# Layer 0's first attention pass written out by itself, and the second group's weights split inside iteration 0

## The chip, the cores and the metric

One core of one Trainium2 chip runs the whole kernel in one launch. The metric is device time in microseconds (us); lower is better. PE is TensorE, DVE VectorE, ACT ScalarE, POOL GpSimd, and SP the engine that issues most transfers. Every engine takes its own instructions strictly in order and waits on semaphores.

## What is computed

Two transformer layers over 4 x 256 tokens of width 256 and a context of 4 x 1601. The change lies in layer 0's attention. Cut to what matters:

```python
ln_out = _ln(hidden_states, ln_w, ln_b)
q  = _ln(fp8_linear(ln_out, wq).reshape(b, s, g, hpg, d))     # 8 groups, 2 heads each, d = 128
k  = _ln(fp8_linear(ln_out, wk).reshape(b, s, g, d))
v  = fp8_linear(ln_out, wv)
core = _gqa(q, k, v)
qx = _ln(fp8_linear(ln_out, wqx).reshape(b, s, g, hpg, d))
kx, vx = split(cond @ w_kv_x.T)                               # 1601 context rows
xout = _gqa(qx, _ln(kx), vx)
catq = _div_clamp_fp8(concatenate([core, xout]), proj_smooth)
out  = (catq @ wproj.T) * (proj_in_scale * proj_w_scale)
```

`fp8_linear` rounds its input to fp8; float32 factors are carried as a high and a low bf16 part.

## The kernel before

Layer 0's attention is 32 iterations (`NGB`), one for each pair of group and batch. The first 16 alternate between batches 0 and 1, so iterations 0 and 1 use group 0, and 2 and 3 use group 1. In iteration `it` the kernel makes the scores and probabilities of `it` and, between them, prepares `it + 1`: queries (`Q0`, `Q1`), keys (`K0` to `K3`), transposed queries (`TQ0`, `TQ1`), sums of squares of the keys (`SS`) and values (`V0` to `V3`). It also multiplies the probabilities of the iteration before by its values. An iteration "-1" has the same order with nothing but the preparation for 0, and work of the start is put between: rounding of the inputs to fp8 (rounds `j` = 0 to 7, four for each of two batches), the split of the second batch's context, and the split of group 1's weights.

Weights. Group 0's lie in `wsb`. Group 1's raw weights `wf1` are split by ACT (high parts, L737), DVE (low parts, L638) and POOL (the context's keys and values, L553 and L555) into `wo`. SP stores `wo` to `w_split` in device memory (`sp_store_weights`, L446), and later loads it into `wsb` in three pieces (`load_weights`, L972): keys (256 KB) and queries (512 KB) for the next iteration but one, values later. PE's first work of iteration 1 is `Q0` of iteration 2, which waits for the piece of the queries:

```python
elif i == 0:
    if new_group(it):
        e.wait_ge(s["ld_q"], 16 * (groups_taken(it) - 1))
```

The load of iteration 2 in turn waits for the store, `e.wait_ge(s["w_out"], 32)`.

The keys' norms. ACT copies `SS` out and issues a small transfer into `ssc`; POOL takes the power -1/2 (`key_norm`, L1110); SP writes that row to device memory (`row_out`, L989) and, once it has landed, reads it back spread over all partitions (`row_in`, L1002), which DVE's scaling of the scores (L1298) needs. SP's other work is the DMA transpose of the probabilities (`turn_p`, L1017).

Rounding. ACT scales (L785), DVE clips and takes exponents (L661, L665, L667) and adds (L672), and DVE or POOL subtracts (L677, L539).

Buffers. PE's products of the preparation go through three banks, `pa` and two of `tb`; `wait_bank` makes a product wait for the reader of the one three slots earlier.

Of the kernel before, what the change touches and what calls it, by code (L numbers as in the profile page):

```python
# [127 lines left out]
def allocate(nc, m, whole):  # L128
# [36 lines left out]
    with ExitStack() as attn:  # L165
# [7 lines left out]
        with ExitStack() as c:  # L173
# [15 lines left out]
            sb(c, "free_turned", [P, IC, NT * P - S], F32)  # L189
            m.wf[1] = sb(c, "wf1", [P, IC, WCOLS], F32)  # L190
            m.wo = sb(c, "wo", [P, 2 * IC * WCOLS], BF16)
        with ExitStack() as c:
# [33 lines left out]
            m.yq = [sb(c, f"yq{i}", [P, 512], BF16) for i in range(2)]  # L226
            m.ye = sb(c, "ye", [P, 512], BF16)
            m.ym = [sb(c, f"ym{i}", [P, 512], BF16) for i in range(2)]
            m.yt = sb(c, "yt", [P, 512], F32)
# [2919 lines left out]
```

## Time and profile before

| | us |
|---|---|
| median of 3 runs | 1675.77 (1675.32 to 1676.99) |
| the profiled execution, and its span | 1673.28, 1671.5 |
| PE busy in the span | 1593.3 (95%) |
| DVE, ACT, POOL busy | 1389.5 (83%), 1387.6 (83%), 1142.2 (68%) |
| PE's first product of iteration 0 (`Q0` of 1) starts at | 59.41 |
| PE busy up to there | 24.24 |
| PE's first product of iteration 1, of 2 and of 3 | 91.00, 123.70, 159.54 |

Times within the trace count from the span's start. "r" in the prediction is time since the start of iteration 0 on PE. A row of the timeline gives start, duration, engine, line, operation, output<-input, shapes and a count; in square brackets is the idle time ahead of it and what ended that.

### The profile page before, as it was taken

What the parts mean: (1) busy time and instruction counts of PE and PEld (TensorE: products, weight loads), DVE (VectorE), ACT (ScalarE), POOL (GpSimd) and SP (SyncE); (2) the same over time, 40 slices, a digit from 0 to 9 for tenths busy, and PEclk for the clock granted to TensorE, in tenths of its full rate; (3) what the DMA queues carried; (4) which work ended last, traced back from release to release, by engine and by line L of the source; (5) the groups of instructions that cost most, each with busy time, mean ns of one, the idle gap of its engine ahead of it and who ended that gap; (6) DMA issues with size and microseconds to landing.
All of it is one profiled execution on the core that took longest, in us unless ns stands there. A gap on an engine that the chain in (4) does not pass through costs nothing. (4 is left out here: it accounts for less than half of the span.)

```text
span 1671.5 us, 44071 instructions
## 1 busy us (share of the span) xinstructions
PE 1593.3 (95%) x15996; PEld 1000.8 (60%) x15996; DVE 1389.5 (83%) x3486; ACT 1387.6 (83%) x2346; POOL 1142.2 (68%) x1775
## 2 busy tenths in 40 slices
PE   3799999999999999999999999998898999999998
PEld 1566777767777677777777677776554333333333
DVE  7899999999999989999988999899896755655422
ACT  6688888888887888888888888885347999999997
POOL 3668778687787777888788888876775655646300
PEclk9899999999999999999999999999999999999999
DMA  5399989899998998999999999999333222222100
GB/s 180 90 200 204 193 197 197 188 203 207 212 192 200 220 208 186 221 217 218 211 196 206 214 210 209 200 182 249 116 51 112 46 54 70 41 40 47 33 14 14
DMA packets 609481, 261.12 MB, mean 156 GB/s; under 512 B 576624, under 2 KB 581744, under 8 KB 607856
## 3 DMA queue, kind: packets, MB, share of 16 engines
q1 hardware_dynamic: 605040, 258.05, 71.6%
q8 instruction: 127, 2.08, 0.5%
q10 hardware_dynamic: 4224, 0.25, 0.2%
q14 instruction: 90, 0.74, 0.1%
HBM read 99.15 MB, written 17.29 MB: 70 GB/s over the span
## 5 line engine op out<-in xcount | busy, mean ns | idle before, releaser
L1815 PE MATMUL score<-KK,QT 128*128 128x512 bf16 (+2 forms) x1920 | 340.7, 321 | 8.1 <-DVE mxp L1298 7.5
L1835 PE MATMUL pv<-PT,VV 128*128 128x256 bf16 (+1 forms) x2880 | 338.8, 274 | 6.5 <-DMA PT<-PB 6.0
L1569 ACT ACTIVATE PB<-S,rsum 128x1024 bf16<-128x1024 f32 (+1 forms) x256 | 246.2, 987 | 109.2 <-DVE rsum L1329 85.0
L1835 PEld LDWEIGHTS pv<-PT,VV 128*128 128x128 bf16 (+1 forms) x2880 | 279.7, 98 | 72.9 <-issue 32.7
L1320 DVE SCALAR_TENSOR_TENSOR PB<-S,rsum,PB 128x1024 bf16<-128x1024 f32 (+1 forms) x256 | 292.2, 1142 | 0.3 <-ACT PB L1569 0.3
L1815 PEld LDWEIGHTS score<-KK,QT 128*128 128x128 bf16 x1920 | 157.0, 98 | 146.8 <-DVE mxp L1298 16.8
L1559 ACT ACTIVATE S<-S,nmx 128x1601 f32<-128x1601 f32 x128 | 210.0, 1641 | 6.4 <-DVE nmx L1310 6.3
L2884 ACT ACTIVATE P<-score 128x1024 f32<-128x1024 f32 x196 | 197.7, 1052 | 1.7 <-PE score L2976 0.8
L2996 PE MATMUL pv<-P,V 128*9 128x256 f32 (+1 forms) x2288 | 152.2, 380 | 1.1 <-DVE pv L2267 0.8
L1694 PE MATMUL tb<-stage,wsb 128*128 128x512 bf16 (+1 forms) x768 | 148.1, 335 | 4.7 <-DVE stage L645 3.9
L1127 POOL TENSOR_SCALAR S<-S,rsum 128x256 f32<-128x256 f32 x128 | 74.4, 581 | 108.8 <-DVE rsum L1329 101.8
L1149 POOL TENSOR_TENSOR catq<-yt,ym 128x512 bf16<-128x512 f32 x64 | 114.9, 1795 | 0.3
L1298 DVE CUSTOM_DVE_ANT_0 S<-score,x 128x1024 f32<-128x1024 f32 (+1 forms) x128 | 104.4, 816 | 6.5 <-PE score L1815 4.5
L1298 DVE CUSTOM_DVE_ANT_0 S<-score,rsb 128x1024 f32<-128x1024 f32 (+1 forms) x128 | 104.5, 816 | 6.2 <-PE score L1815 2.9
L1694 PEld LDWEIGHTS tb<-stage,wsb 128*128 128x128 bf16 x768 | 66.2, 98 | 70.0 <-issue 6.6
L1513 ACT ACTIVATE kn<-pa,a_nm,a_rs 128x128 f32<-128x128 f32 x256 | 95.7, 455 | 8.0 <-POOL a_nm L1090 8.0
L1085 POOL TENSOR_SCALAR a_nm<-a_mv 128x4 f32<-128x4 f32 x64 | 41.8, 653 | 88.3 <-DVE a_mv L1264 88.3
L1735 PE MATMUL tb<-wsb,stage 128*128 128x128 bf16 x1536 | 98.7, 222 | 3.0 <-DVE KK L1231 2.8
L1139 POOL TENSOR_TENSOR yt<-yq,ym 128x512 f32<-128x512 bf16 x64 | 91.4, 1428 | 14.4 <-DVE ym L1354 9.6
L1131 POOL TENSOR_TENSOR PB<-S,PB 128x256 bf16<-128x256 f32 x128 | 90.3, 705 | 10.9
L1735 PEld LDWEIGHTS tb<-wsb,stage 128*128 128x128 bf16 x1536 | 93.2, 99 | 7.2 <-DVE KK L1231 5.2
L2976 PE MATMUL score<-QB,KT 32*128 32x256 bf16 (+1 forms) x1110 | 91.0, 274 | 4.5 <-ACT P L2884 2.5
(295 smaller groups left out, 3671.7 us busy)
## 6 DMA issues: line engine op xcount, KB each, us to landing
x<-rs_d SPq DMA_DIRECT2D x16, 936.0 KB, 5.2
rsb<-rs_d SPq DMA_DIRECT2D x16, 936.0 KB, 5.5
wsb<-w_split SPq DMA_DIRECT2D x46, 256.0 KB, 4.7
wsb<-w_split SPq DMA_DIRECT2D x23, 512.0 KB, 4.9
wpr<-in_wprojT SPq DMA_DIRECT2D x23, 512.0 KB, 6.6
context_d<-stage SPq DMA_DIRECT2D x16, 400.2 KB, 4.1
l_ctx<-context_d SPq DMA_DIRECT2D x4, 1601.0 KB, 7.3
rawh<-in_w_all SPq DMA_DIRECT2D x12, 512.0 KB, 5.5
```

The source lines that it names most:

```text
L1149: e.tensor_tensor(out[:, :, pr * 256:(pr + 1) * 256], m.yt[:, :].rearrange("p (k c) -> p k c", k=2), m.ym[pr][:, :].rearrange("p (k c) -> ...
L1298: e.tensor_tensor_reduce(m.S32[par][:, at:at + b - a], m.score[:, a:b], m.rsb[it % 2][:, key:key + b - a], 1.0, start, ALU.mult, ALU.max, ...
L1320: e.scalar_tensor_tensor(m.PB[n % 2][:, lo:lo + b - a], m.S32[n % 2][:, a:b], m.rsum[n % 2][:, 1:2], m.PB[n % 2][:, 2 * a:a + b], ALU.mult ...
L1513: a = e.activation(m.kn[i][:, k * D:(k + 1) * D], bank[:, k * D:(k + 1) * D], ACT.Identity, bias=m.anm[i][:, k:k + 1], scale=m.ars[i][:, k ...
L1559: e.activation(x, x, ACT.Exp, bias=m.nmx[par][:, 1:2], accum_out=m.sums[par][:, 1:2])
L1569: e.activation(m.PB[n % 2][:, 2 * a:a + b], m.S32[n % 2][:, a:b], ACT.Copy, scale=m.rsum[n % 2][:, 1:2]).then_inc(s["p_hi"], 1)
L1694: r = e.matmul(bank[:, 0:b - a], wk[:, w, ic, D:2 * D], ctx_op(m, it, part, ic, a, b), start=(n == 0), stop=(n == 5))
L1735: r = e.matmul(bank[:, h * D:(h + 1) * D], ctx_op(m, it, part, ic, t * P, (t + 1) * P), wv[:, w, ic, D:2 * D], start=(n == 0), stop=(n == 5))
L1815: i = e.matmul(m.score[:, at:at + b - a], qt[:, kind, qp, q * P:(q + 1) * P], kk[:, kp, a:b], start=(k == 0), stop=(k == 2))
L1835: i = e.matmul(m.pv[:, at:at + 256], vv[0:rows, v, t, :], m.PT[k % 2][0:rows, turned(c, a), :], start=(c == first and r == 0), stop=(c == ...
L2884: e.activation(pr[:, :], bank, ACT.Exp, scale=float(D1) ** -0.5).then_inc(s["l1_exp"], 1)
L2996: r = e.matmul(m.pv[j * R:j * R + VC, 0:S], m.V1[p][0:rows, t, 4 * hq + j, :], probabilities(m, n, j // 2)[0:rows, at:at + S], start=(t == ...
```

## The change

Iteration -1 goes. In its place each engine has a list of its own for the first pass. ACT and DVE split both halves of the first context before they scale or round any input. PE makes `K0` and `K1` first, then `Q0`, `K2`, `K3`, transposes the rest of the tokens, and puts `SS` directly behind the keys; POOL's root and the row's way over device memory follow. Rounds 5, 6 and 7, and the whole split of group 1's weights, move into iteration 0. SP stores `wo` there behind the row of iteration 1, and then loads iteration 2's keys' and queries' weights. Four small buffers move in the memory map, since `wo` now lives longer; waits in iteration 1 guard their first use. The core of the diff:

```diff
@@ allocate
+            m.yq = [sb(c, f"yq{i}", [P, 512], BF16) for i in range(2)]
+            m.ye = sb(c, "ye", [P, 512], BF16)
+            m.ym = [sb(c, f"ym{i}", [P, 512], BF16) for i in range(2)]
+            m.yt = sb(c, "yt", [P, 512], F32)
             m.ast = [sb(c, f"a_st{i}", [P, 4, 6], F32) for i in range(2)]
...
@@ pool_prologue
+    for i in range(2):
+        e.memset(m.S32[i][:, SC:SELFC], 0.0).then_inc(s["p_pad"], 1)
...
+    pool_round_end(e, m, s, 1)
@@ dve_prologue
     dve_weights_low(e, m, s, 0, 1)
-    dve_round(e, m, s, 0)
     dve_context_low(e, m, s, 0, 0)
-    dve_round(e, m, s, 1)
     dve_context_low(e, m, s, 0, 1)
-    dve_weights_low(e, m, s, 0, 2)
     e.wait_ge(s["x_rest"], 16)
     dve_statistics(e, m, s, 1, m.x, TB, NT)
...
+    dve_round(e, m, s, 0)
@@ act_prologue
+    act_context_high(e, m, s, 0, 0)
+    act_context_high(e, m, s, 0, 1)
     act_scaled_inputs(e, m, s, 0)
-    act_context_high(e, m, s, 0, 0)
     act_scaled_inputs(e, m, s, 1)
-    act_context_high(e, m, s, 0, 1)
     act_weights_high(e, m, s, 0, 2)
-    act_scaled_inputs(e, m, s, 2)
     act_weights_high(e, m, s, 0, 3)
-    act_scaled_inputs(e, m, s, 3)
...
+FIRST = ("K0", "K1", "Q0", "K2", "K3", "SS", "TQ0", "V0", "Q1", "V1", "TQ1", "V2", "V3", "PR")
...
-    at = ORDER.index(what)
+    at = (ORDER if it else FIRST).index(what)
@@ sp_attention
-    for it in range(-1, NGB + LAG - 1):
-        if it == -1:
-            sp_store_weights(e, m, s, 1)
-        if it == 0:
-            sp_small(e, m, s)
+    row_out(0)
+    row_in(0)
+    sp_small(e, m, s)
+
+    for it in range(NGB + LAG - 1):
...
-        load_weights(it + 2, 0)
+        if it:
+            load_weights(it + 2, 0)
...
-        if it + 2 < PAIRS:
+        if 0 < it < PAIRS - 2:
             load_weights(it + 2, 1)
         row_out(it + 1)
         row_in(it + 1)
+        if it == 0:
+            sp_store_weights(e, m, s, 1)
...
         turn_p(4 * it + 1, 1)
+        if it == 0:
+            load_weights(2, 0)
+            load_weights(2, 1)
@@ pool_attention
-    for it in range(-1, NGB + LAG - 1):
-        if it == 0:
-            e.wait_ge(s["xq_done"], 8)
...
+    query_norm(0, 0)
+    pool_round_end(e, m, s, 2)
+    pool_context_low(e, m, s, 1, 0)
+    key_norm(0)
+    query_low(0, 0)
+    query_norm(0, 1)
+    pool_round_end(e, m, s, 4)
+    pool_context_low(e, m, s, 1, 1)
+    query_low(0, 1)
+
+    for it in range(NGB + LAG - 1):
...
+        if it == 0:
+            pool_round_end(e, m, s, 5)
+            pool_split_weights(e, m, s, 1, 0)
+            pool_round_end(e, m, s, 6)
         split_self(4 * it)
         query_norm(it + 1, 1)
         query_low(it + 1, 0)
-        if it == -1:
-            pool_split_weights(e, m, s, 1, 0)
-            pool_round_end(e, m, s, 4)
+        if it == 0:
+            pool_round_end(e, m, s, 7)
             pool_split_weights(e, m, s, 1, 1)
...
         key_norm(it + 1)
...
+        if it == 1:
+            e.wait_ge(s["w_out"], 32)
@@ dve_attention
+        if it == 0:
+            dve_round_start(e, m, s, 5)
+            dve_round_add(e, m, s, 5)
...
+        if it == 0:
+            dve_round_start(e, m, s, 6)
+            dve_round_add(e, m, s, 6)
+        if it == 1:
+            e.wait_ge(s["w_lo_pool"], 8)
...
+        if it == 0:
+            dve_weights_low(e, m, s, 1, 0)
         invert(4 * it)
...
+        if it == 0:
+            dve_weights_low(e, m, s, 1, 1)
...
+        if it == 0:
+            dve_round_start(e, m, s, 7)
+            dve_round_add(e, m, s, 7)
...
+        if it == 0:
+            dve_weights_low(e, m, s, 1, 2)
+            dve_weights_low(e, m, s, 1, 3)
         values_low(it + 1, 0)
@@ act_attention
+    keys_high(0, 0)
+    act_scaled_inputs(e, m, s, 2)
+    keys_high(0, 1)
+    act_normalise_rest(e, m, s)
+    keys_high(0, 2)
+    keys_high(0, 3)
+    act_scaled_inputs(e, m, s, 3)
+    query_norm(0, 0)
+    act_context_high(e, m, s, 1, 0)
+    sums_out(0)
+    query_full(0, 0)
...
+        if it == 0:
+            act_scaled_inputs(e, m, s, 6)
...
+        if it == 0:
+            act_weights_high(e, m, s, 1, 0)
+            act_scaled_inputs(e, m, s, 7)
...
+        if it == 0:
+            act_weights_high(e, m, s, 1, 1)
         p_hi(4 * it, 0)
...
+        if it == 0:
             act_weights_high(e, m, s, 1, 2)
             act_weights_high(e, m, s, 1, 3)
+        query_norm(it + 1, 1)
@@ pe_attention
+        if n == 0 and half == 0:
+            e.wait_ge(s["xw_done"], 2 * IC)
...
+    keys(0, 0)
+    keys(0, 1)
+    queries(0, 0)
+    keys(0, 2)
+    keys(0, 3)
+    pe_turn_normed(e, m, s, 1)
+    squares(0)
+    turn_queries(0, 0)
+    values(0, 0)
+    queries(0, 1)
+    values(0, 1)
+    turn_queries(0, 1)
+    values(0, 2)
+    values(0, 3)
```

PE's order at the start of the program, before. `score<-ident,xn` is the transposition of normalised tokens, `pa<-wsb,stage` queries, `tb<-stage,wsb` keys, `tb<-sq,ones` the sums of squares, `tb<-wsb,stage` values:

```order
L831 MATMUL score<-ident,xn 128x128 x4
L1768 MATMUL pa<-wsb,stage 128x256 x8
L1694 MATMUL tb<-stage,wsb 128x512 x12
L831 MATMUL score<-ident,xn 128x128 x12
L1779 MATMUL pa<-ident,kn 128x128 x4
L1694 MATMUL tb<-stage,wsb 128x512 x6
L1694 MATMUL tb<-stage,wsb 128x65 x6
L1702 MATMUL tb<-stage,wsb 128x256 x4
L1768 MATMUL pa<-wsb,stage 128x256 x8
L1716 MATMUL tb<-sq,ones 32x480 x4
L1735 MATMUL tb<-wsb,stage 128x128 x48
```

And of the change:

```order
L825 MATMUL score<-ident,xn 128x128 x4
L1725 MATMUL tb<-stage,wsb 128x512 x12
L1799 MATMUL pa<-wsb,stage 128x256 x8
L1725 MATMUL tb<-stage,wsb 128x512 x6
L1725 MATMUL tb<-stage,wsb 128x65 x6
L1733 MATMUL tb<-stage,wsb 128x256 x4
L825 MATMUL score<-ident,xn 128x128 x12
L1747 MATMUL tb<-sq,ones 32x480 x4
L1810 MATMUL pa<-ident,kn 128x128 x4
L1766 MATMUL tb<-wsb,stage 128x128 x24
L1799 MATMUL pa<-wsb,stage 128x256 x8
```

The keys moved ahead of the queries, and the squares ahead of the second queries and of all transposed queries and values.

SP's order from the store of group 0's weights on, before (`x<-rs_d` and `rsb<-rs_d` are the rows of iterations 0 and 1 read back):

```order
L446 DMA w_split<-wsb 128x4096
L446 DMA w_split<-wo 128x4096
L989 DMA rs_d<-rr 128x15
L1002 DMA x<-rs_d 128x1872
...
L972 DMA wsb<-w_split 128x1024
L1017 DMA_TRANSPOSE PT<-PB 128x14x128
L1017 DMA_TRANSPOSE PT<-PB 128x16x128 x2
L972 DMA wsb<-w_split 128x2048
L989 DMA rs_d<-rr 128x15
L1002 DMA rsb<-rs_d 128x1872
L1017 DMA_TRANSPOSE PT<-PB 128x14x128
```

And of the change, up to where iteration 1's transposes begin:

```order
L446 DMA w_split<-wsb 128x4096
L984 DMA rs_d<-rr 128x15
L997 DMA x<-rs_d 128x1872
...
L1012 DMA_TRANSPOSE PT<-PB 128x14x128
L1012 DMA_TRANSPOSE PT<-PB 128x16x128 x2
L984 DMA rs_d<-rr 128x15
L997 DMA rsb<-rs_d 128x1872
L446 DMA w_split<-wo 128x4096
L1012 DMA_TRANSPOSE PT<-PB 128x14x128
L967 DMA wsb<-w_split 128x1024
L967 DMA wsb<-w_split 128x2048
```

The store of `wo` moved from ahead of iteration 0's row to behind iteration 1's, and both loads of `wsb` moved behind the store.

POOL's order from the second queries' norm of iteration 1 to the root of its keys, before (`wo` and `acc` are the split weights of groups 1 and 2, `stage<-late,ex` the end of a round, `rr<-ssc,mhalf` the root):

```order
L1090 TENSOR_TENSOR a_nm<-a_nm,a_rs 128x4
L1099 CAST QT<-t 128x512
L1101 TENSOR_TENSOR QT<-t,QT 128x512
L553 CAST acc<-rawh 128x128
L555 TENSOR_TENSOR acc<-rawh,acc 128x128
...
L1131 TENSOR_TENSOR PB<-S_1,PB 128x256
L1110 TENSOR_TENSOR rr<-ssc,mhalf 128x15
```

And of the change:

```order
L1091 TENSOR_TENSOR a_nm<-a_nm,a_rs 128x4
L1100 CAST QT<-t 128x512
L1102 TENSOR_TENSOR QT<-t,QT 128x512
L539 TENSOR_TENSOR stage<-late,ex 128x512
L553 CAST wo<-wf 128x128
L555 TENSOR_TENSOR wo<-wf,wo 128x128
L553 CAST wo<-wf 128x128
L555 TENSOR_TENSOR wo<-wf,wo 128x128
L553 CAST acc<-rawh 128x128
L555 TENSOR_TENSOR acc<-rawh,acc 128x128
...
L1132 TENSOR_TENSOR PB<-S_1,PB 128x256
L1111 TENSOR_TENSOR rr<-ssc,mhalf 128x15
```

One end of a round and one part of the split of `wo` now stand between the queries and the root.

## Rows read from the trace of the kernel before

**Rows 1.** Windows: busy time by engine in iterations 0 and 1, then clock, DMA.
```profile
59.41:91.00 31.59, 27.18 (x230) 17.64 (x231) 26.83 (x79) 25.82 (x61) 18.26 (x29) 0.95 0.54 122
91.00:123.70 32.70, 32.59 (x299) 23.31 (x297) 29.92 (x76) 27.14 (x53) 18.48 (x24) 1.00 1.00 204
```

**Rows 2.** Timeline, PE: first keys, a value, first queries of iterations 0, 1.
```profile
21.86 4.16 PE L1694 MATMUL tb<-stage,wsb 128*128 128x512 bf16 x12 [3.94 <-DVE stage L645]
...
49.10 2.74 PE L1735 MATMUL tb<-wsb,stage 128*128 128x128 bf16 x24 [0.20 <-ACT sqs L1534]
...
59.41 1.89 PE L1768 MATMUL pa<-wsb,stage 128*128 128x256 bf16 x8 [4.00 <-DVE VV L1244]
...
91.00 1.04 PE L1768 MATMUL pa<-wsb,stage 128*128 128x256 bf16 x8
```

**Rows 3.** Groups of lines, ACT, 0 to 62.3 us.
```profile
L765 ACT CAST stage<-cf 128x1601 bf16<-128x1601 f32 x4 | 6.1, 1524 | 0.0
L785 ACT ACTIVATE stage<-xr,rin 128x256 bf16<-128x256 f32 x8 | 3.6, 504 | 0.0
...
L737 ACT ACTIVATE wo<-wf,win 128x256 bf16<-128x256 f32 (+1 forms) x8 | 3.1, 461 | 0.0
L793 ACT ACTIVATE xn<-x,rr,rs 128x256 f32<-128x256 f32 x6 | 3.1, 587 | 0.7 <-POOL rr L586 0.7
L1513 ACT ACTIVATE kn<-pa,a_nm,a_rs 128x128 f32<-128x128 f32 x8 | 3.0, 457 | 3.3 <-POOL a_nm L1090 3.3
```

**Rows 4.** The landing times of the contexts' transfers (`cf`).
```profile
DMA to landing us min/median/max: 4.2/5.5/8.2
```

**Rows 5.** Groups of lines, POOL, 0 to 62.3 us.
```profile
L562 POOL TENSOR_TENSOR stage<-cf,stage 128x577 bf16<-128x577 f32 x4 | 5.7, 1428 | 5.0 <-ACT stage L765 5.0
L539 POOL TENSOR_TENSOR stage<-late,ex 128x512 bf16<-128x512 f32 x3 | 3.5, 1154 | 1.0 <-DVE late L672 1.0
L1110 POOL TENSOR_TENSOR rr<-ssc,mhalf 128x15 f32<-128x15 f32 x1 | 2.7, 2749 | 0.0
L1101 POOL TENSOR_TENSOR QT<-t,QT 128x512 bf16<-128x512 f32 x2 | 2.4, 1182 | 0.2
L1088 POOL TENSOR_TENSOR a_rs<-a_rs,mhalf 128x4 f32<-128x4 f32 x2 | 2.2, 1080 | 0.2
...
L555 POOL TENSOR_TENSOR wo<-wf,wo 128x128 bf16<-128x128 f32 x4 | 2.1, 516 | 0.3
```

**Rows 6.** Groups of lines, DVE, 0 to 62.3 us.
```profile
L672 DVE TENSOR_TENSOR late<-stage,ex 128x512 f32<-128x512 bf16 x8 | 5.5, 693 | 0.3
...
L638 DVE SCALAR_TENSOR_TENSOR wo<-wf,win,wo 128x256 bf16<-128x256 f32 (+1 forms) x8 | 4.1, 556 | 0.0
```

**Rows 7.** Timeline, ACT, in iteration 0.
```profile
64.57 0.69 ACT L1485 ACTIVATE KK<-tb,dcols 128x512 bf16<-128x512 f32 x1 [7.78 <-PE tb L1694]
65.15 0.59 ACT L1490 ACTIVATE sq<-tb 128x512 f32<-128x512 f32 x1
...
72.03 1.86 ACT L1569 ACTIVATE PB<-S,rsum 128x1024 bf16<-128x1024 f32 x2
```

**Rows 8.** Timeline, DVE: statistics of the second queries in iteration 0.
```profile
73.75 0.89 DVE L1258 BATCH_NORM_STATS2 a_st<-pa 128x6 f32<-128x128 f32 x4 [0.58 <-PE pa L1768]
```

**Rows 9.** Timeline, POOL: root of iteration 1's keys.
```profile
84.09 2.76 POOL L1110 TENSOR_TENSOR rr<-ssc,mhalf 128x15 f32<-128x15 f32 x1
```

**Rows 10.** Timeline, SP's queue: row of iteration 1 out and in.
```profile
86.88 0.32 SPq L989 DMA_DIRECT2D rs_d<-rr  x1
90.38 0.32 SPq L1002 DMA_DIRECT2D rsb<-rs_d  x1
```

**Rows 11.** DMA issues, 0 to 100 us: size, us to landing.
```profile
w_split<-wo SPq DMA_DIRECT2D x1, 1024.0 KB, 3.9
...
rsb<-rs_d SPq DMA_DIRECT2D x1, 936.0 KB, 5.4
...
wsb<-w_split SPq DMA_DIRECT2D x1, 512.0 KB, 4.4
```

More of the change, by code:

```diff
@@ L225, in allocate @@
             m.rsum = [sb(c, f"rsum{i}", [P, 2], F32) for i in range(2)]
[L226 to L229, printed above, removed]
             m.rawh = sb(c, "rawh", [P, IC, 512], F32)[:, :, :]
@@ L1150, in take_magnitudes @@
                         m.ym[pr][:, :].rearrange("p (k c) -> p k c", k=2), ALU.subtract).then_inc(s["yq_done"], 1)
-    for it in range(-1, NGB + LAG - 1):
-        if it == 0:
-            e.wait_ge(s["xq_done"], 8)
-            for i in range(2):
-                e.memset(m.S32[i][:, SC:SELFC], 0.0).then_inc(s["p_pad"], 1)
+    query_norm(0, 0)
[8 more added lines that the diff above has]
+    for it in range(NGB + LAG - 1):
         query_norm(it + 1, 0)
@@ L1355, in exponents @@
                         ALU.add).then_inc(s["y_mag"], 1)
-    for it in range(-1, NGB + LAG - 1):
+    keys_low(0, 0)
+    dve_round_start(e, m, s, 1)
+    dve_round_add(e, m, s, 1)
+    keys_low(0, 1)
+    query_stats(0, 0)
+    dve_weights_low(e, m, s, 0, 2)
+    dve_round_start(e, m, s, 2)
+    dve_round_add(e, m, s, 2)
+    keys_low(0, 2)
+    keys_low(0, 3)
+    dve_weights_low(e, m, s, 0, 3)
+    dve_round(e, m, s, 3)
+    e.tensor_scalar(m.gate[:, 0:1], m.gate[:, 0:1], sc(m, "pw"), sc(m, "pin"), ALU.mult, ALU.mult)
+    e.reciprocal(m.rsmc[:, :], m.smc[:, :])
+    dve_context_low(e, m, s, 1, 0)
+    dve_sum_weights(e, m, s, 1)
+    dve_centre_weights(e, m, s, 1)
+    query_stats(0, 1)
+    values_low(0, 0)
+    dve_round_start(e, m, s, 4)
+    dve_round_add(e, m, s, 4)
+    values_low(0, 1)
+    dve_context_low(e, m, s, 1, 1)
+    values_low(0, 2)
+    values_low(0, 3)
+    for it in range(NGB + LAG - 1):
         query_stats(it + 1, 0)
@@ L1570, in p_hi @@
             s["p_hi"], 1)
-    for it in range(-1, NGB + LAG - 1):
+    keys_high(0, 0)
[9 more added lines that the diff above has]
+    query_full(0, 0)
+    for ic in range(IC):
+        act_norm_weighted(e, m, s, ic)
+    act_scaled_inputs(e, m, s, 4)
+    values_high(0, 0)
+    values_high(0, 1)
+    act_context_high(e, m, s, 1, 1)
+    query_norm(0, 1)
+    query_full(0, 1)
+    values_high(0, 2)
+    values_high(0, 3)
+    act_scaled_inputs(e, m, s, 5)
+    for it in range(NGB + LAG - 1):
         if it == 0:
             e.wait_ge(s["p_pad"], 3)
-            e.wait_ge(s["w_lo_dve"], 16)
-            e.wait_ge(s["w_lo_pool"], 8)
+            e.wait_ge(s["w_lo_dve"], 8)
+            e.wait_ge(s["w_lo_pool"], 4)
             e.wait_ge(s["ctx_lo_dve"], 2 * IC)
             e.wait_ge(s["ctx_lo_pool"], 2 * IC)
-            e.wait_ge(s["xq_done"], 8)
         p_hi(4 * it - 1, 0)
         keys_high(it + 1, 0)
-        if it == -1:
-            act_context_high(e, m, s, 1, 0)
-            act_normalise_rest(e, m, s)
+        if it == 0:
+            act_scaled_inputs(e, m, s, 6)
         if it < NGB - 1:
@@ L1837, in times_v @@
         i.then_inc(s["tv_done"], 1)
-    for it in range(-1, NGB + LAG - 1):
+    keys(0, 0)
[12 more added lines that the diff above has]
+    values(0, 3)
+    for it in range(NGB + LAG - 1):
         queries(it + 1, 0)
```

66 lines of the change are left out of this document (3 added, 63 removed).

## The prediction

> **What bounds the kernel now.** I read the windows first. From iteration 1 on PE is the bound: it is busy 32.59 of 32.70 us there [rows 1], so whatever moves the start of iteration 1 moves the end by as much. Two stretches are not PE's: everything up to 59.41, where PE's first product of iteration 0 starts [rows 2], and iteration 0 itself, where PE works 27.18 of 31.59 us and DVE 26.83, ACT 25.82 [rows 1]. The time before is thus 59.41 + 31.59 + the rest, and the whole question is when `Q0` of iteration 2, which starts at 91.00 [rows 2], can start now. Next I read the timelines of both stretches, engine by engine, and last the transfers, because the code makes that product wait for one.
>
> **The first pass: when does iteration 0 start?** No duration changes, so I lay the new lists out by hand along the chain that ends last.
> - Contexts. The later of them lands 8.2 us after its issue at about 4.1 to 4.5 [rows 4], so at 12.5. The cast takes 1.5 [rows 3] and POOL's upper half of the low part 1.4 [rows 5]: `K0` starts at 15.4, where it started at 21.86 [rows 2]. `K0` and `K1` take 4.2 together [rows 2], to 19.6.
> - ACT then has `K1`'s high part and square (0.7 and 0.6 [rows 7]) to 20.9, the normalisation of the other tokens 3.1 [rows 3] to 24.0, two more pairs for `K2` and `K3` (2.3) to 26.3, a scaling 0.9 [rows 3] to 27.2, the queries' norm 1.5 and a context's cast 1.5 [rows 3] to 30.2, and the copy of the sums, about 0.6 as one such square, to 30.8. (This last row is the one that used to come behind the second queries.)
> - The small transfer of the sums lands some 2.5 later: such a row took at most 3.5 from its issue until the next could go [rows 10], and I take a little less. POOL's root takes 2.75 [rows 5]: 33.3 to 36.0.
> - POOL then writes the first queries (0.6 + 1.2, by the cast's half and the row of 1.18 [rows 5]) to 37.8 and takes the root for the second (a power of 1.08 [rows 5] and three tiny ones, 2.0) to 39.8. ACT normalises them by 41.3, PE transposes, ACT scales, and PE's third value of up to 2.74 [rows 2] ends near 44.4; its high and low part take 0.6 and 0.7.
> This puts `Q0` of iteration 1 at 45.3: 14.1 us earlier than 59.41. The value at the higher clock gives 44.5, a slower context (5.5 from its issue is the median, 8.2 the slowest, so it is not likely) or 1 us of contention on POOL 47. POOL and ACT are both nearly full between 20 and 40, so I don't expect less than 44.
>
> **Iteration 0 gets longer.** Moved in are, on ACT, two scalings (3.6 us for four [rows 3], so 1.8) and the high parts of `wo`, 3.1 [rows 3]; on DVE, three rounds of four steps, 0.69 for the last [rows 6] and near 1.0 for the other three, 1.7 each, less the round of 2.4 that ran at its start, and the low parts, 4.1 with contention [rows 6]; on POOL, three ends of rounds at 1.15 and two splits at 1.7 (0.52 and about 0.35, twice [rows 5]). ACT was idle 7.78 us, but only until `K0` of iteration 1 [rows 7], and nothing that moved stands there but one scaling: the rest lies behind it, where ACT had no gap.
> - ACT reaches the high parts of the probabilities, which began at r = 72.03 - 59.41 = 12.6 [rows 7], after two scalings and two parts of the weights: 0.9 + 0.9 + 0.9 + 0.7 = 3.4 later, r 16.0.
> - DVE's low part of the second piece waits for ACT just ahead of that, to r 16. Its statistics of the second queries, at r 14.3 [rows 8], then come at r 18.3: 4.0 later.
> - POOL's root of iteration 1's keys hangs on those statistics through a chain without a gap. It ended at 84.09 + 2.76 = 86.85, r 27.4 [rows 9]. Now 4.0 later for DVE, and an end of a round (1.15) and a split (1.7) stand ahead of it: r 34.3; I take 33.8, for some contention falls away.
> - PE itself would reach `Q0` of iteration 2 at r 37.5, where it was at 31.6: the values wait for DVE's last low part of the keys, which waits for ACT.
> So without any transfer in the way iteration 0 costs 5.9 more and the change wins 14.1 - 5.9 = 8.2 us.
>
> **But the reload is late.** Before, both pieces of `wsb` were loaded during iteration 0. Now SP issues, in this order: the row out behind the root, the row in, the store of `wo`, a transpose, and only after the store has landed the keys' and queries' weights. From the end of the root, K = 45.3 + 33.8 = 79.1:
> - row out to row in: 3.5 [rows 10]
> - row in to the store's issue: 0.4; the store alone lands in 3.9 [rows 11], but 936 KB of the row, 5.4 us to landing [rows 11], go ahead of it through the same DMA engines. It lands between 3.9 and about 7 after its issue (5.4 and some 2 for its own bytes); I take 5.9.
> - two issues, 0.4 for the second; the 512 KB of the queries' weights land in 4.4 [rows 11], with the transpose ahead of them.
> Sum: 3.5 + 0.4 + 5.9 + 0.4 + 4.4 = 14.6, between 12.6 with the store alone and 15.7 with the row and 7.0 for the store; a transpose of some 2 us in front gives 18. `Q0` of iteration 2 starts at 79.1 + 14.6 = 93.7. PE would be ready at 45.3 + 37.5 = 82.8 and stands still for 10.9 us. Queued behind that product are all of iteration 1's scores, so nothing fills the hole. 93.7 - 91.0 = 2.7 later than before.
>
> The Trainium skill (DMA: Bandwidth & Descriptors, "Anatomy of one DMA") puts a transfer at 2.0 us fixed and its bytes at 436 GB/s. By this estimate row, row and store together, and both loads take 2.0 + 0.4 + 6.6 + 0.4 + 3.8 = 13.2 instead of 14.6, and the sum of the change would be 1.4 less; for the store alone it gives 4.4, where the trace has 3.9 [rows 11], and no row shows a store behind a row. The same page's rules for kernel authors ask that a transfer be issued early and waited for late; this change does the opposite with the store and the loads.
>
> **The clock.** After 4.0 us idle the eight products at 59.41 took 1.89, and at 91.00, behind a busy PE, 1.04 [rows 2]: 0.85 lost in that group alone. After 10.9 us idle the slow stretch is longer; two to three times 0.85 is 1.7 to 2.6. I take 1.8.
>
> Sum: +2.7 + 1.8 = +4.5 us. The other edits cost nothing: the waits of iteration 1 are for things then long done (the store landed before PE could go on), the memsets moved into POOL's idle start. The profiled execution took 1673.28, 2.5 below the median; its terms hold for both. Median 1675.77 + 4.5 = 1680.3.
>
> **Rivals.**
> 1. The reload is in time (faster): the change does what its first pass promises. It needs the queries' weights landed by 82.8, when PE comes; from `Q0` at 91.0 - 1.8 - 3.4 = 85.8 on it is no longer measurably faster. It would happen if POOL's root came at once with its sums (spans on POOL are rough, and it has 13 us idle of 31.59 before [rows 1]): K at r 26, 71.3, and the short chain of 12.6 give 83.9. Against it: POOL's list puts two splits and a round ahead of the root. 1667.6 at best, 1671 in the middle.
> 2. A wash: the store lands in its 3.9 beside the row, and K is 1 us early: 78.1 + 12.6 = 90.7, -0.3 + 1.8 = +1.5, 1677.3. For it: DMA engines are half idle in iteration 0 (0.54 [rows 1]). Against it: the row and the store follow within 0.4 us.
> 3. Worse: the transpose and the row both hold the path, 18 us from K, and iteration 0 starts at 46.5: 98.3, +7.3 + 2.6 = +9.9, 1685.7.
> 4. The stall gives something back: ACT, DVE and the DMA catch up in it, and PE's few waits of iterations 2 and 3 vanish. At most 1 to 2 us, since PE was busy 32.59 of 32.70 just behind [rows 1]; it is inside the range.
>
> **How the numbers follow.** Forecast (stall of about 11 us, +2.5 to +7): 0.50. Rival 2 (-3 to +2.5): 0.26. Rival 3: 0.08. Rival 1: 0.16. A change of 0.2% (3.4 us) is about what can be told from none. The likeliest case alone runs from 1678 to 1683. The range takes in rival 2 and parts of 1 and 3: 1671.5 to 1686. Slower by over 0.2%: two thirds of the forecast's case and more, and rival 3: 0.52. Within: 0.31. Faster: 0.17.
>
> **What would show it.** PE's first keys near 15.4 and the squares near 28; `Q0` of iteration 1 near 45; POOL's root of iteration 1 near 79; an idle of 8 to 14 us ahead of PE's `Q0` of iteration 2, ended by the transfer `wsb<-w_split`, at 92 to 96; the lower clock behind it; from there on the same distances as before. The prediction is wrong if that idle is under 3 us, or if iteration 0 starts later than 49.

## The result, and the profile after

The changed kernel takes 1681.54 us (median of 6 runs, 1678.66 to 1683.66) where the kernel before took 1675.34 beside it (6 runs, 1673.41 to 1676.99). The ratio is 1.0037, with a 95% interval of 1.0027 to 1.0048: slower by 6.2 us. The profiled execution has a span of 1679.6 us.

The windows of the first pass, of iteration 0 and of iteration 1 (span of the window, busy time of PE, PEld, DVE, ACT and POOL, granted clock, DMA share, GB/s), which answer to [rows 1]:

```profile
0.00:47.65 47.65, 20.87 (x162) 14.20 (x163) 37.02 (x97) 30.31 (x58) 29.08 (x53) 0.93 0.50 190
47.65:96.08 48.43, 28.90 (x230) 18.36 (x231) 35.48 (x98) 34.77 (x81) 27.41 (x37) 0.80 0.44 104
96.08:130.90 34.82, 34.81 (x296) 24.16 (x297) 27.68 (x70) 23.48 (x47) 18.99 (x24) 0.93 0.73 145
```

The first pass is 11.76 us shorter than its 59.41 [rows 2]. Iteration 0 is 16.84 longer than its 31.59, iteration 1 2.12 longer than its 32.70 [rows 1]. Both engines that took on work are far from full in iteration 0 (ACT 34.77 of 48.43 us), so it is not their load that fills it. TensorE's timeline has the reason (start, busy time, then in brackets the idle time ahead and what ended it), against [rows 2]:

```profile
16.62 5.28 PE L1725 MATMUL tb<-stage,wsb 128*128 128x512 bf16 x12 [8.69 <-POOL stage L562]
...
42.60 1.09 PE L1810 MATMUL tb<-ident,kn 128*128 128x128 f32 x4 [6.14 <-ACT kn L1536]
...
47.65 1.05 PE L1799 MATMUL pa<-wsb,stage 128*128 128x256 bf16 x8 [0.54 <-DVE VV L1249]
...
96.08 1.86 PE L1799 MATMUL pa<-wsb,stage 128*128 128x256 bf16 x8 [11.75 <-DMA wsb<-w_split]
97.74 2.76 PE L1848 MATMUL score<-KK,QT 128*128 128x512 bf16 x6
100.30 1.76 PE L1725 MATMUL tb<-stage,wsb 128*128 128x512 bf16 x6
```

The rows at 47.65 and 96.08 are `Q0` of iterations 1 and 2. TensorE is through with everything else at 96.08 - 11.75 = 84.33, which is 6.7 us earlier than it was at this place before, and then stands still for the weights. After the pause the same products run at about half speed (six scores take 2.76 instead of 1.46). From `Q0` of iteration 3 on, at 130.90, the distances are those of before: `Q0` of iteration 5 stands at 201.44, against 194.32.

SP's queue in iteration 0 shows the chain in front of that load, and the landings of its transfers (size, median us from issue to landing) what it is made of; compare [rows 10, 11]:

```profile
80.70 0.36 SPq L984 DMA_DIRECT2D rs_d<-rr  x1
82.16 0.33 SPq L997 DMA_DIRECT2D rsb<-rs_d  x1
82.65 0.32 SPq L446 DMA_DIRECT2D w_split<-wo  x1
83.07 5.62 SPq L1012 DMA_TRANSPOSE PT<-PB  x1
90.86 0.80 SPq L967 DMA_DIRECT2D wsb<-w_split  x2
...
w_split<-wo SPq DMA_DIRECT2D x1, 1024.0 KB, 8.1
rsb<-rs_d SPq DMA_DIRECT2D x1, 936.0 KB, 6.1
...
wsb<-w_split SPq DMA_DIRECT2D x1, 512.0 KB, 4.7
```

The store of `wo` leaves at 82.65 and lands 8.1 us later; alone, before the change, it landed in 3.9 [rows 11]. Only then may the loads go.

And POOL's last piece of `wo`, and the root that SP's row waits for:

```profile
74.06 0.49 POOL L555 TENSOR_TENSOR wo<-wf,wo 128x128 bf16<-128x128 f32 x1
...
77.87 2.80 POOL L1111 TENSOR_TENSOR rr<-ssc,mhalf 128x15 f32<-128x15 f32 x1
```

POOL's share of the split is ready at 74.6, DVE's at 75.0. So the store stands for over 7 us behind the row in SP's list, with its data ready. SP's waits between 60 and 100 us name the root as what the row waited for; the root ends at 80.67 and the row leaves at 80.70:

```profile
SPq L984 <- POOL rr L1111: 3.2, 1, 3.2
```

### The profile page after: what moved, and what is told of

Its sections match the earlier page's. It is cut to its first block and busy times, and to the rows that moved or that the text cites. A ratio compares the mean times of both kernels' runs of the same rounds, so it can differ in the third digit from the quotient of the medians.

```text
span 1679.6 us, 44073 instructions
## 1 busy us (share of the span) xinstructions
PE 1595.2 (95%) x15996; PEld 1001.1 (60%) x15996; DVE 1384.2 (82%) x3483; ACT 1386.4 (83%) x2346; POOL 1151.1 (69%) x1778
## 5 line engine op out<-in xcount | busy, mean ns | idle before, releaser
L1508 ACT ACTIVATE KK<-tb,dcols 128x512 bf16<-128x512 f32 (+1 forms) x128 | 76.1, 594 | 31.1 <-PE tb L1725 31.1
L1132 POOL TENSOR_TENSOR PB<-S,PB 128x256 bf16<-128x256 f32 x128 | 93.6, 731 | 10.9
```

## Experiments

Theory A: the chain row, store, loads in front of iteration 2's first queries is the loss; without it the first pass's gain would come through, less what iteration 0 has taken on. Rivals: TensorE would wait for something else there (B); iteration 0 is too long by its new work (C); the new first pass is worth little by itself (D).

All kernels side by side. `Q0(1)` and `Q0(2)` are the starts of those queries in the profiled execution, "wait" is TensorE's idle time ahead of the second; iteration 1 is from `Q0(2)` to `Q0(3)`. The ratio is against the kernel before on the same chip.

| kernel | Q0(1) | Q0(2) | wait | iteration 1 | median us | ratio, 95% interval |
|---|---|---|---|---|---|---|
| before | 59.41 | 91.00 | 0 | 32.70 | 1675.34 | 1 |
| changed | 47.65 | 96.08 | 11.75 | 34.82 | 1681.54 | 1.0037 [1.0027, 1.0048] |
| e1 store early | 47.66 | 91.89 | 7.25 | 34.97 | 1676.86 | 1.0007 [0.9998, 1.0016] |
| e10 and loads ahead of row_in | 48.75 | 90.97 | 4.79 | 34.87 | 1675.50 | 0.9995 [0.9986, 1.0005] |
| e2 copies inside SBUF | 48.79 | 85.28 | 0 | 35.61 | 1669.67 | 0.9963 [0.9951, 0.9976] |
| e4 second store | 47.49 | 98.10 | 13.98 | 35.04 | 1683.60 | 1.0054 [1.0039, 1.0069] |
| e5 root first | 48.87 | 97.44 | 11.55 | 34.79 | 1682.05 | 1.0036 [1.0023, 1.0049] |
| e3 split in the first pass | 48.72 | 83.17 | 0 | 32.32 | 1667.84 | 0.9952 [0.9939, 0.9964] |
| e6 and rounds 5 to 7 too | 49.64 | 84.97 | 0 | 32.31 | 1667.78 | 0.9954 [0.9942, 0.9967] |
| e7 is e3, norm first | 48.12 | 81.97 | 0 | 32.31 | 1664.54 | 0.9935 [0.9923, 0.9948] |
| e8 is e7, keys first | 47.96 | 82.97 | 0 | 32.41 | 1664.83 | 0.9931 [0.9918, 0.9945] |
| e11 is e6, norm first | 49.20 | 85.64 | 0 | 32.31 | 1666.95 | 0.9951 [0.9939, 0.9963] |
| e9 76 products in the wait | 48.88 | 97.67 | 3.79 | 34.00 | 1684.51 | 1.0058 [1.0044, 1.0073] |
| e12 104 products in the wait | 48.96 | 98.17 | 0.22 | 32.71 | 1684.18 | 1.0067 [1.0048, 1.0086] |

**e1, the store early.** In iteration 0 of SP's list:

```diff
+        if it == 0:
+            sp_store_weights(e, m, s, 1)
         row_out(it + 1)
         row_in(it + 1)
         if it == 0:
-            sp_store_weights(e, m, s, 1)
+            load_weights(2, 0)
+            load_weights(2, 1)
...
         turn_p(4 * it + 1, 1)
-        if it == 0:
-            load_weights(2, 0)
-            load_weights(2, 1)
```

> Only SP's order in iteration 0 changes: the 1 MB store of the second group's weights goes ahead of row_out(1), and the two loads for iteration 2 directly behind row_in(1), ahead of the fourth transpose. Theory A (the chain row, store, loads holds TensorE for 11.75 us in front of iteration 2's first queries, and with the lower clock behind it costs 13 to 14 us): the split is whole at about 75 us and SP is past its third transpose at 77.5 us, so the store leaves at about 77.5 instead of 82.65, lands alone in about 4 us, and the loads go out at about 83 instead of 90.86; those queries start at 88 to 89 instead of 96.08, and the time is 1672 to 1675 us. Rival B (the later store only trades its wait for another one of the same engine, for instance the squares' chain of iteration 1): less than 2 us of it, 1679 to 1681.

SP's queue and the landings in e1:

```profile
77.64 0.83 SPq L446 DMA_DIRECT2D w_split<-wo  x1
80.70 0.33 SPq L984 DMA_DIRECT2D rs_d<-rr  x1
84.14 0.32 SPq L997 DMA_DIRECT2D rsb<-rs_d  x1
84.56 0.85 SPq L967 DMA_DIRECT2D wsb<-w_split  x2
...
w_split<-wo SPq DMA_DIRECT2D x1, 1024.0 KB, 6.3
...
wsb<-w_split SPq DMA_DIRECT2D x1, 512.0 KB, 6.8
```

The store left 5.0 us sooner, as expected. But it took 6.3 instead of 4, the row behind it landed in 3.4 instead of 1.4, and the larger of the loads, now behind the broadcast row, took 6.8. Of the 5 us 4.5 came off the wait. The 7 to 8 us and the 1672 to 1675 that were expected are missed, because the durations were taken as if no other transfer were under way. The median fell by 4.7: about one for one with the wait.

**e10, the loads ahead of the row's broadcast.** As e1, with `load_weights(2, 0)` and `load_weights(2, 1)` between `row_out` and `row_in`.

> The kernel with the early store (1676.9; TensorE waited 7.25 us, the two loads took 5.0 and 6.8 us behind the row's 936 KB broadcast), with the two loads ahead of row_in(1). If the broadcast in front of the loads costs what it seems to, the loads leave at about 84 us and take 4 to 5 us, TensorE's wait is 4.5 to 5.5 us and the time 1674 to 1675.5. If the store's own landing (6.3 us beside the transposes) sets it, under 0.7 us is won and the time stays at 1676 to 1677.5.

The larger load landed in 4.9 instead of 6.8 and the wait fell by 2.5 to 4.79, as expected. The time fell by only 1.4 us and its interval overlaps that of e1. In the profiled execution the first pass is 1.1 us longer than in e1, so `Q0(2)` itself is only 0.9 sooner (the last section has the two lengths of that pass). The direction is right, the size not settled.

**e2, copies inside SBUF.** The weights that iteration 2 needs first don't go through DRAM; the store stays behind the row, for the others:

```diff
+        if it == 0:
+            wait_split(e, s, 1, False)
+            for which, name, last in ((0, "ld_k", "K3"), (1, "ld_q", "Q1")):
+                e.wait_ge(s["pa_full"], made(1, last))
+                a, b = w_at[which], w_at[which + 1]
+                e.dma_start(m.wsb[:, a:b], m.wo[:, a:b]).then_inc(s[name], 16)
         row_out(it + 1)
```

> The keys' and queries' halves of iteration 2's weights are copied from the split tile wo to wsb inside SBUF, at about 77.5 us, ahead of the row; the store of wo to DRAM stays where it was and no longer stands in front of anything that iteration 2 needs first. Theory A: both copies have landed by 83 us, TensorE is ready for iteration 2's first queries at 84.3 us and starts them there with a wait under 1 us, so 11.75 us of idle time and 1 to 2 us of lower clock go: 1667 to 1670 us. Rival B (TensorE would have stood still for something else at that place, the squares or DVE's statistics): the wait keeps 4 us or more under another name and the time is 1673 or more. Rival C (the lengthening of iteration 0 by rounds 5 to 7 and the splits is the main cost): no more than 3 us are won, 1678 or more.

SP's queue in e2, and from TensorE's timeline `Q0` of iteration 2 and a wait for P:

```profile
78.89 1.36 SPq L1058 DMA_DIRECT2D wsb<-wo  x2
81.83 0.36 SPq L984 DMA_DIRECT2D rs_d<-rr  x1
84.42 0.33 SPq L997 DMA_DIRECT2D rsb<-rs_d  x1
84.92 0.32 SPq L446 DMA_DIRECT2D w_split<-wo  x1
```

```profile
85.28 1.04 PE L1809 MATMUL pa<-wsb,stage 128*128 128x256 bf16 x8
...
94.69 2.46 PE L1878 MATMUL pv<-PT,VV 128*128 128x256 bf16 x21 [1.59 <-DMA PT<-PB]
```

The wait is gone and nothing took its place: rivals B and C fall. The time is 12 us under the changed kernel and 6 under the one before. What is left of the store shows in iteration 1: 35.61 us at full clock, 2.9 more than before. One piece is the 1.59 us for a transposed P; whether it is late because its transpose stands behind the store and the row was not tested apart.

**e4, a second store.** After `sp_store_weights(e, m, s, 1)`:

```diff
+            e.dma_start(m.w_spare, m.wo[:, :]).then_inc(s["w_out"], 16)
```

and every wait on `w_out` from there on asks for 16 more.

> A second store of the same 1 MB, to a spare tensor, stands behind the first and the loads wait for both. Theory A: TensorE's wait grows by what a second megabyte takes behind the first, 2 to 4 us, one for one, 1683 to 1686 us. Rival E (that store's 8.1 us landing is a latency behind the broadcast row and not the data): the second megabyte adds under 1 us, 1681 to 1682.5.

```profile
w_split<-wo SPq DMA_DIRECT2D x1, 1024.0 KB, 7.9
w_spare<-wo SPq DMA_DIRECT2D x1, 1024.0 KB, 10.1
```

These are both stores, the second issued 0.4 us behind the first; it lands 2.5 us behind it. A megabyte more costs 2.2 us of wait (13.98 for 11.75). The ratio rises by 0.0017, 2.8 us, but the two intervals overlap. So bytes on this chain are on the path, and rival E falls as far as the wait tells. The first megabyte's 7.9 is for the most part not its own bytes. In the trace of the changed kernel the row's packets (7488 bytes each) start between 83.1 and 87.6 us and the store's (8192 bytes each) between 87.2 and 90.1, though the store was issued at 82.65.

**e5, the root first.** On POOL in iteration 0 `key_norm(1)` goes ahead of `pool_split_weights(2, 1)` and `split_self(1)`.

> The changed kernel with one thing moved on POOL in iteration 0: the root of iteration 1's row (key_norm(1)) goes ahead of the first part of group 2's split (about 1.5 us) and of one P residue (about 1.8 us). Theory A (the row's root K heads the chain root, row_out, row_in, store, loads, first queries of iteration 2): the root ends at about 77.5 instead of 80.67 us, each step behind it comes 3 us sooner, TensorE's wait falls from 11.75 to 8.5 to 9 us, and the time falls by 2.5 to 4 us against the changed kernel: 1677 to 1679. Rival (the store's place among the transposes sets it, the root has slack): TensorE's wait stays over 11 us and the time at 1680.5 to 1682.

The root, SP's queue and SP's wait for the row's landing in e5 (`Q0(1)` is 1.22 us later in this execution, so these times are to be read less 1.22):

```profile
75.75 2.79 POOL L1111 TENSOR_TENSOR rr<-ssc,mhalf 128x15 f32<-128x15 f32 x1
...
71.97 6.85 SPq L1012 DMA_TRANSPOSE PT<-PB  x3
78.86 0.82 SPq L984 DMA_DIRECT2D rs_d<-rr  x1
83.18 0.33 SPq L997 DMA_DIRECT2D rsb<-rs_d  x1
83.67 0.32 SPq L446 DMA_DIRECT2D w_split<-wo  x1
...
rs_d<-rr SPq DMA_DIRECT2D x1, 7.5 KB, 4.3
...
SPq L997 <- DMA rs_d<-rr: 3.4, 1, 3.4
```

Here theory A failed as I had stated it: an earlier root wins nothing. It ends 3.3 us earlier and the row leaves 3.1 us earlier, but its 7.5 KB, now directly behind three transposes, take 4.3 us to land instead of 1.4: they land at 81.9 after the correction, and in the changed kernel at 82.1. The store leaves at 82.45 after the correction, instead of 82.65, and the wait is 11.55.

What holds the row is not the same in the two kernels. The last of the three transposes was issued at 75.17 in the changed kernel and at 76.31 in e5, and these are their landings:

```profile
PT<-PB SPq DMA_TRANSPOSE x1, 6.2
...
PT<-PB SPq DMA_TRANSPOSE x1, 6.7
```

In e5 that transpose lands at 83.0 and the row 0.2 behind it, at 83.2. In the changed kernel it lands at 81.4 and the row 0.7 behind it, 1.44 us after its own issue at 80.70. There the DMA engines had nothing to move just before (last two numbers: their share and GB/s):

```profile
79.60:81.50 1.90, 1.19 (x10) 0.54 (x8) 1.61 (x4) 1.90 (x5) 1.82 (x3) 1.00 0.00 0
```

So in the changed kernel the root does head the chain, and the transposes are the next limit, half a microsecond behind (81.4 + 0.2 against 82.1). An earlier root can win no more than that before it runs into them. The same 0.2 us recurs wherever the transfer ahead of the row is still under way. In e1 the store lands at 83.95 and the row at 84.13, in e10 they land at 85.50 and 85.69, and before the change the 512 KB load lands at 90.2 and the row at 90.4. No run took the transposes away. The Trainium skill (DMA: Bandwidth & Descriptors, "Queues, rings and completion order") says that each DMA engine consumes the descriptors of one queue in ring order. The landings of e5, e1 and e10 agree with it; the row of the changed kernel, whose own 1.44 us end later than the transposes, neither supports nor contradicts it.

**e3, the split back in the first pass.** On ACT, DVE and POOL the four, four and two pieces of group 1's split stand in the new first pass, for instance on ACT

```diff
     act_context_high(e, m, s, 1, 1)
+    act_weights_high(e, m, s, 1, 0)
+    act_weights_high(e, m, s, 1, 1)
     query_norm(0, 1)
+    act_weights_high(e, m, s, 1, 2)
     query_full(0, 1)
+    act_weights_high(e, m, s, 1, 3)
     values_high(0, 2)
```

the store stands behind `sp_small`, and the loads for iteration 2 at their old places.

> The change's new first pass, with the second group's split put back into it on all three engines, its store back behind the small transfers, and the loads for iteration 2 back at their places of before; rounds 5 to 7 of the inputs stay in iteration 0. This is the first-pass half of the change alone. Theory A: the pass ends 1 to 2 us later than 47.65, iteration 0 falls back to 33 to 34 us from 48.4, no wait for wsb is left: iteration 2's first queries start at 82 to 83 us, 8 to 9 us ahead of the kernel before, and the time is 1665 to 1669 us. Rival D (the earlier first pass is given back anyway, because iteration 0 waits for data that come no sooner than before): 1673 to 1676.

```profile
83.17 1.04 PE L1789 MATMUL pa<-wsb,stage 128*128 128x256 bf16 x8
```

Everything as theory A has it, but for the first pass: it ends 1.07 us later than in the changed kernel, and no later than in e2, e5 and e9, whose first pass has no split in it (48.79 to 48.88; the last section comes to these two lengths). So the split costs the pass nothing that can be told from these two lengths. Iteration 0 takes 34.45, iteration 1 32.32. The median is 7.5 us under the kernel before, 13.7 under the changed one. Rival D falls: the earlier first pass is not given back.

**e6, rounds 5 to 7 in the first pass as well.** What is left of the change is the order of the first pass.

> Both the second group's split and rounds 5 to 7 of the inputs stand in the first pass again; what is left of the change is the new order of the first pass alone (contexts and keys first, squares and root directly behind). If rounds 5 to 7 had been free in iteration 0, they now cost the first pass 2 to 4 us (it ends at 51 to 53 us) and iteration 0 falls to about 32 us, as before the change: the first queries of iteration 2 stand at 83 to 85 us and the time is 1667 to 1670, equal to or slightly over the 1667.8 of the kernel with only the split put back. Rival (the new order gains little by itself, the gain is the rounds' move): the pass ends at 56 or later and the time is 1672 or more.

The time came as forecast, 1667.78, equal to e3. Its parts didn't: the pass ends at 49.64 and iteration 0 takes 35.33, not 32. The window behind the pass, and the waits that open it, in e6:

```profile
49.64:65.72 16.08, 13.77 (x74) 7.07 (x77) 13.85 (x39) 7.58 (x16) 7.55 (x14) 0.90 0.29 100
```

```profile
49.64 1.89 PE L1782 MATMUL pa<-wsb,stage 128*128 128x256 bf16 x8 [2.44 <-DVE VV L1242]
```

DVE comes late out of the fuller pass, TensorE waits for it (2.44, 0.31, 0.73, and 0.99 for ACT's `kn`) and begins at the lower clock (1.89 for the eight products, 1.05 in e3): 16.08 us from the first to the second queries, where e3 takes 12.20. So moving the rounds and leaving them cost the same, and the gain of the change is the order of the first pass alone.

**e7, e8, e11: better than both.** e7 is e3 with one exchange on POOL, e8 adds the keys ahead of P in iteration 0, e11 is e6 with e7's exchange:

```diff
     key_norm(0)
-    query_low(0, 0)
     query_norm(0, 1)
+    query_low(0, 0)
```

> The kernel with the split back in the first pass (1667.8), with POOL's query_norm(0, 1) put ahead of query_low(0, 0). There ACT waited 1.66 us for a_nm and TensorE 7.35 us for kn in front of the second turn. If POOL's order holds that chain, a_nm comes 1.9 us sooner, the first pass ends 1 to 1.9 us sooner, and the time is 1666 to 1667. If ACT's or DVE's own queue holds it, less than 0.5 us changes.

> The kernel before this one, and in iteration 0 alone ACT takes the last block of iteration 1's keys ahead of the first two parts of P, and DVE likewise. There TensorE waited 2.36 us for the squares and 2.48 us for the bank that DVE empties. If these waits end what they seem to, iteration 0 is 2 to 3 us shorter and the time 1663.5 to 1665.5. Rival: P, now later, makes the transposes and TensorE's P times V late by the same amount, and nothing is won or 1 us lost.

> The new first pass with the split and rounds 5 to 7 both in it (1667.8), and with query_norm(0, 1) ahead of query_low(0, 0) on POOL, which was worth 3.3 us where only the split stood in the pass (1664.5). There the pass ended with a wait of 2.44 us for DVE, and the first stage of iteration 0 ran at a granted clock of 0.90. If the order on POOL is what held the end of the pass, 2 to 3 us come off again: 1664.5 to 1666. If DVE, fuller here by rounds 5 to 7 (15.4 busy of 15.6 us), holds it, under 1 us: 1667 to 1668.

In e7 the second turn (the transposition of the second queries, `tb<-ident,kn`) starts at 41.53 instead of e3's 43.67 (and the changed kernel's 42.60), the pass ends 0.6 us sooner than in e3, and `Q0(2)` stands 1.2 us earlier. The ratio, 0.9935, is 2.8 us better than e3's, more than the trace explains and more than was expected (1666 to 1667), and the two intervals overlap. e8 is a miss: the squares' wait of 2.37 shrinks to 0.61, but `V0` waits 2.69 instead of 1.67 for the same bank, and TensorE waits 1.97 instead of 1.64 for P's transpose and then runs at a granted clock of 0.62 (between 78.6 and 83.1 us), 4.45 us where e7 has 2.78:

```profile
78.68 4.45 PE L1865 MATMUL pv<-PT,VV 128*128 128x256 bf16 x24 [1.97 <-DMA PT<-PB]
```

The waits only changed places, and the clock took the rest: nothing is won, 1664.83. e11's gain of 0.8 us is of the size of the noise; the pass ended 0.44 sooner with a wait for DVE of 2.91 instead of 2.44, so there DVE holds the end, not POOL. The best kernels of the study are e7 and e8, which can't be told apart; e7 takes 1664.54 us, 0.65% under the kernel before.

**e9 and e12, the clock.** Ahead of iteration 2's first queries, in the same bank:

```diff
+        if it == 2 and i == 0:
+            for n in range(76):
+                e.matmul(bank[:, 0:256], xq_op(m, 1, 0, n % IC, 0, P), xq_op(m, 1, 1, n % IC, 0, 256), start=True, stop=True)
```

> The changed kernel with 76 idle products (128x256, each into the bank that the first queries of iteration 2 overwrite) put in front of those queries, 8 to 10 us of work in a wait of 11.75 us, which stays. Theory A (about 2 us of the loss is TensorE's clock at half its level after the wait): the first queries start where they did (r about 48.4 us after iteration 1's) but take 1.04 instead of 1.86 us, iteration 1 lasts 32.7 to 33 us instead of 34.8, and the time is 1679 to 1680 us, 1.5 to 2 us under the changed kernel. Rival (iteration 1 is longer because V and the transposes are late behind the same loads): it still lasts 34 us or more and the time stays at 1681 to 1682.

> As the kernel with 76 idle products, with 104. The 76 ran 0.112 us each and ended 3.79 us ahead of the loads' landing; after that gap the first queries still ran at full speed (1.05 us), but the scores and keys behind them took 2.48 and 2.17 us instead of 1.46, and iteration 1 lasted 34.0 us. 104 products end at most 0.7 us ahead of the landing. If the clock behind the wait answers to TensorE's own idle time, scores and keys take 1.46 us and iteration 1 lasts 32.5 to 33 us. If it answers to something else (the DMA load, which is the same), they stay over 2 us and the iteration at 34. No forecast of the whole time better than 1679.5 to 1683.

TensorE in e9, then in e12:

```profile
85.36 8.52 PE L1789 MATMUL pa<-stage 128*128 128x256 bf16 x76
97.67 1.05 PE L1802 MATMUL pa<-wsb,stage 128*128 128x256 bf16 x8 [3.79 <-DMA wsb<-w_split]
98.55 2.48 PE L1851 MATMUL score<-KK,QT 128*128 128x512 bf16 x6
100.82 2.17 PE L1725 MATMUL tb<-stage,wsb 128*128 128x512 bf16 x6
```

```profile
86.30 11.65 PE L1789 MATMUL pa<-stage 128*128 128x256 bf16 x104
98.17 1.05 PE L1802 MATMUL pa<-wsb,stage 128*128 128x256 bf16 x8 [0.22 <-DMA wsb<-w_split]
99.27 1.24 PE L1851 MATMUL score<-KK,QT 128*128 128x512 bf16 x5
```

With the hole filled iteration 1 takes 32.71 us, to 0.01 what it took before the change; the loads and the transfers beside them are as late as in the changed kernel. So the 2.12 us of iteration 1 are the clock and nothing else, and it is TensorE's own idle time that lowers it. In e9 a hole of 3.79 us was enough to lose 1.30 of them. From there the loss doesn't grow with the hole: iteration 1 takes 34.87, 34.97, 34.82 and 35.04 us behind waits of 4.79 (e10), 7.25 (e1), 11.75 and 13.98 us (e4). The whole time answered otherwise than expected: 1684.51 and 1684.18, some 3 us above the changed kernel where 1.5 to 2 below it were forecast for e9. So no median shows that the 2.1 us come back at the end of the kernel. e12's `Q0(2)` is 2.1 us late to begin with (1.3 from the first pass, 0.8 more in iteration 0); that is just made good by the clock, and at `Q0(5)` it stands 0.20 ahead of the changed kernel (201.24, 201.44). It is 1.25 ahead at the changed kernel's `Q0` row at 701.80 and 2.63 behind at the one at 755.75. Between them lies a wait for DVE, among others (TensorE in e12):

```profile
735.76 0.36 PE L1725 MATMUL tb<-stage,wsb 128*128 128x65 bf16 x6 [1.32 <-DVE KK L1239]
```

Why DVE slipped there, and whether it does in every execution, stays open.

## Why the prediction was right

The forecast was +4.5 us, at 1680.3; measured were +6.2 and 1681.54. By its steps:

- **TensorE is the bound from iteration 1 on, so `Q0` of iteration 2 tells the end.** Right over e4, e5, the changed kernel, e1 and e10: `Q0(2)` at 98.10, 97.44, 96.08, 91.89 and 90.97 gave 1683.6, 1682.1, 1681.5, 1676.9 and 1675.5. e9 and e12 don't fit: with `Q0` of iteration 3 at 131.67 and 130.88, against 130.90 in the changed kernel, they take 3.0 and 2.6 us more than it.
- **The first pass ends at 45.3.** It ended at 47.65, 2.35 later, and this is the whole error of `Q0(2)` (93.7 forecast, 96.08 measured). 1.2 of it stood at `K0`: POOL's two pieces of the context's low part took 4.46 us together, 2.2 each where 1.4 was taken, so `K0` began at 16.62. The rest came on the way to `Q0` of iteration 1; 0.4 of it stands in the prediction's own sum, where 44.4 and the two parts of 0.6 and 0.7 make 45.7 if they don't overlap. POOL's order made part of it: one exchange put e7's turn at 41.53, 1.1 us ahead of the changed kernel's 42.60.
- **Iteration 0 is 5.9 longer for TensorE itself.** 84.33 - 47.65 = 36.68, against 31.59: 5.1 longer. e3 divides it: 2.9 with the rounds there, 2.2 more with the split. The total is near, but its steps were off in both directions. ACT reached the high parts of the probabilities at r 14.0 instead of 16.0 and DVE the statistics at r 16.5 instead of 18.3. From there to the end of the root POOL needed 16.5 us where 15.5 were taken; one end of a round took it 1.74 instead of 1.15 and one piece of the split 1.51 instead of 0.52. The prediction had contention fall away there. That the root came at r 33.0 for 33.8 is luck in part.
- **K to `Q0(2)` 14.6.** Measured 96.08 - 80.67 = 15.4: row out to row in 1.5 instead of 3.5, the store 8.1 instead of 5.9, the loads 5.2 with their issue instead of 4.8. The two errors in the row and the store nearly cancel, which is luck, and r of the root takes up the rest. The row's 3.5 had been read where the row stood behind a load of 512 KB that was still under way; with nothing under way it took 1.44. The store's two parts added up instead of overlapping: its bytes moved only when the row's were through. "The root heads the chain" was right, but only half a microsecond ahead of the transposes, as e5 showed; the prediction had only asked what a transpose in front would cost. What the Trainium skill (DMA: Bandwidth & Descriptors, "Anatomy of one DMA") gives, 2.0 us and the bytes at 436 GB/s, is its fit for transfers that GpSimd issues; here SP issued them. The prediction's estimate by it, 13.2, was 2.2 short.
- **A stall of about 11 us in front of `Q0(2)`, ended by the load.** 10.9 forecast, 11.75 measured; e2 takes it away and wins 12 us, e4 adds 2.2 to it.
- **The clock costs 1.8.** Mis-sized a little: 2.1 in iteration 1, shown by e12. Its working, that a longer pause makes a longer slow stretch, did not show: waits of 4.79 to 13.98 us cost 2.1 to 2.3 us alike.
- **Nothing fills the hole.** Right in iteration 1: it runs the 32.70 of before, plus the clock. Rival 4 (something given back later) is seen in neither; e12 lost, if anything.
- **Rival 1 (the reload in time)** gives 1667.6 to 1671 in the forecast; e2, where the weights are in time, took 1669.67. With the split in iteration 0 and its way through DRAM no run reached it: with the store directly behind the third transpose, e1 and e10 still wait 7.25 and 4.79 us.

Where the expected gain went, in one sum: the first pass gave 11.8, iteration 0's work took 5.1, the stall 11.75, the clock 2.1: +7.2 at `Q0(3)`, and 6.2 in the medians.

## What to carry to other kernels

Before moving work under cover of a busy engine, follow its result to the next one who needs it: here the split itself cost iteration 0 2.2 us, and its way through DRAM behind a row 11.75. Here a transfer of a few KB landed with the one still under way ahead of it; an earlier producer buys nothing until the queue ahead of it is shorter. A step can head the chain and still be worth nothing when it is made faster, if the next limit stands close behind it. And price a transfer by what stands ahead of it in its queue: the same megabyte took 3.9, 6.3 and 8.1 us here.
